# Second feed-forward of a fused graph network: 64-column scan matrices, pooling sums inside the value products, slice transposes in two banks

## The chip, the cores and the metric

The kernel runs on one core of a Trainium2 chip. The time is the device time of one execution in microseconds (us). Of the engines, TensorE (PE) makes matrix products and transposes, with weight loads (PEld) that overlap them; VectorE (DVE) and ScalarE (ACT) do elementwise work and read PE's results from eight PSUM banks; GpSimd (POOL) makes a few elementwise operations; SyncE (SP) issues transfers.

## The reference

Four layers, each a graph part and a feed-forward part, run over 32 graphs of 256 nodes with 128 features, all in fp32. The change lies in the feed-forward of the third layer (L2). For each graph, rows are softly assigned to 64 slices per head; the slices' means pass a two-way state-space scan (Hydra), and are spread back to the rows:

```python
sw = softmax((xm @ W_slice.T + b_slice) / temp)        # rows x 64 slices, 8 heads
snorm = sw.sum(2)
st = einsum('bhnc,bhng->bhgc', fx, sw) / (snorm + 1e-05)[..., None]
...                                                    # Hydra over the 64 slices of one graph:
h = h * dA_t[:, :, None, None] + dBx_t                 # forward, and on the flipped sequence
y = pad(y_fw[:, :-1], ((0, 0), (1, 0), (0, 0))) + pad(y_bw[:, 1:], ((0, 0), (0, 1), (0, 0)))
y = y + x_og * repeat(x_og @ fcD_w.T + Dp, P, axis=-1)
yg = y * silu(z)
yg = yg * rsqrt(mean(square(yg), -1, keepdims=True) + 1e-05) * norm_w
ot = yg @ out_w.T
out = einsum('bhgc,bhng->bhnc', ot, sw) @ out_w.T + out_b
```

No scan couples two graphs.

## The kernel before

`phase_ffn2` handles 512 rows, two graphs, in a turn; 16 turns (`every_turn`: the first two and the last two written out, the rest a loop of two). Every engine has a program of its own in written order, tied by semaphores; nothing is reordered. In a turn's program work of three turns is interleaved: the scan of turn t, the tail of turn t-1 (`tail_y`, `tail_o`, `tail_p`, `fin_piece`) and the softmax of turn t+1 (`to_features`, `lg_piece`, `soft_a`, `exp_piece`, `soft_b`).

The 128 partitions of a token tile are the 64 slices of graph a and the 64 of graph b. The scan is computed as a matrix: `dt_run` (dt times a mask, per direction) goes through a product with the masks (D, L2377, banks 6 and 7), exponentials (L2214) and a product with `factor` into `decay`, a 128x128 matrix per head of which only the two blocks of a row's own graph are not zero. `decay` times the tokens `xtok` gives y (L2387, bank 5).

Order on PE in a turn: `pool_h` (L2289), which waits for the previous turn's `yg`; `tail_y`; `pool_sums` for graph 0 (product with ones L2294 for the sums, value products L2296); `to_features`; `pool_sums` for graph 1; `tail_o` (L2263); `lg_piece` 0 (L2240); then z (L2332), which waits for `stT`; `lg_piece` 1; x (L2338); the rest of the projection; `lg_piece` 2, `tail_p`, `lg_piece` 3; `fin_piece` (L2282) and `swT_piece` (transposes of the slice weights, L2249, all through bank 0, evacuated by ACT L2145) in turns; the transposes of `xT` (L2363); G (L2368) and fcd (L2370); D; `swT_piece` 2, `fin_piece` 3; y; `swT_piece` 3.

Order on DVE: `pooled` for each graph (L2000, L2002, L2006); `soft_a` 0 (L1985), `soft_b` 0, `soft_a` 1, `sz`, `soft_b` 1; the convolution taps (L2020, L2026); the softplus of dt; `xT`, `Bt`, `Cpad`; `soft_a` 3; `dt_run` backward (L2086; ACT makes the forward one, L2203); `dt_both`, `gm`, `g8`, `g_both`, `factor` (L2098); `soft_b` 2; `decay` (L2104); the residual of turn t-1; the sum with `term` (L2110); `yg` (L2111); `soft_b` 3; `yn`.

Of the kernel before, what the change touches and what calls it, by code (L numbers as in the profile page):

```python
# [26 lines left out]
P = 128  # L27
# [1823 lines left out]
def phase_ffn2(nc, c):  # L1851
# [13 lines left out]
    LG = (B[3], B[2])  # L1865

# [8 lines left out]
    with ExitStack() as ctx:  # L1875
# [3 lines left out]
        def sem(n):  # L1879
# [9 lines left out]
        logit_w, value_w = sb("logit_w", [P, IN2]), sb("value_w", [P, IN2])  # L1889
        sn = sb("sn", [P, 2, KC, SL])  # L1890
# [9 lines left out]
        gm, g_both = sb("gm", [P, 2, P]), sb("g_both", [P, P])  # L1900
        xtok = sb("xtok", [P, IN2])

        dt_run = [sb(f"dt_run{i}", [P, HEADS2, P]) for i in range(2)]
        dt_both, factor = sb("dt_both", [P, HEADS2, P]), sb("factor", [P, HEADS2, P])
        decay = [c.spare["ffn2"][:, q * 4 * P:(q + 1) * 4 * P].rearrange("p (h t) -> p h t", h=4) for q in range(2)]
# [18 lines left out]
        with nc.Block() as block:  # L1924
            @block.gpsimd
            def _(g):
                def turn(t, par, first, last):
# [4 lines left out]
                    g.wait_ge(norm_ps, t * 2 + 1)  # L1932
# [10 lines left out]
            def _(v):  # L1943
# [30 lines left out]
                v.scalar_tensor_tensor(value_w[:], w["b_fx"], last_row, B[4][:], ALU.mult, ALU.add).then_inc(fused, 1)  # L1974
# [59 lines left out]
                def turn(t, par, first, last):  # L2034
# [3 lines left out]
                    pooled(t, 0)  # L2038
                    pooled(t, 1)
# [58 lines left out]
                    v.tensor_tensor(factor[:], dt_both[:], g_both[:, None, :].broadcast_to([P, HEADS2, P]), ALU.mult).then_inc(factor_ready, 1)  # L2098
# [26 lines left out]
            def _(a):  # L2125
# [43 lines left out]
                def turn(t, par, first, last):  # L2169
# [56 lines left out]
            def _(pe):  # L2226
# [84 lines left out]
                def turn(t, par, first, last):  # L2311
# [22 lines left out]
                    if more:  # L2334
                        lg_piece(t + 1, 1)
# [1130 lines left out]
```

## Time and profile before

| | us |
|---|---|
| runs | 3245.23, 3245.34, 3250.94; median 3245.34 |
| span of the profiled execution | 3243.7 |
| PE busy in the span | 2606.3 |
| DVE busy | 2274.7 |
| ACT busy | 1783.4 |
| a steady turn of this stage (14 of 16 are alike but for the clock) | 41.3 |

The profile's times count from the first instruction. The profiled execution is one by itself, whose only time is its span, 1.6 us under the runs' median. PE's busy time is modelled at a product's end, so a group's length holds the last product's tail. In a turn the distance between the same instruction of two turns is the cost of a turn; what the distance consists of has to be read from the waits between engines.

### The profile page before, as it was taken

What the parts mean: (1) busy time and instruction counts of PE and PEld (TensorE: products, weight loads), DVE (VectorE), ACT (ScalarE), POOL (GpSimd) and SP (SyncE); (2) the same over time, 40 slices, a digit from 0 to 9 for tenths busy, and PEclk for the clock granted to TensorE, in tenths of its full rate; (3) what the DMA queues carried; (4) which work ended last, traced back from release to release, by engine and by line L of the source; (5) the groups of instructions that cost most, each with busy time, mean ns of one, the idle gap of its engine ahead of it and who ended that gap; (6) DMA issues with size and microseconds to landing.
All of it is one profiled execution on the core that took longest, in us unless ns stands there. A gap on an engine that the chain in (4) does not pass through costs nothing. (4 is left out here: it accounts for less than half of the span.)

```text
span 3243.7 us, 68706 instructions
## 1 busy us (share of the span) xinstructions
PE 2606.3 (80%) x19386; PEld 2087.8 (64%) x19386; DVE 2274.7 (70%) x6679; ACT 1783.4 (55%) x5130; POOL 867.6 (27%) x863
## 2 busy tenths in 40 slices
PE   5899996992776941789999999699996888759992
PEld 4577776992675941656776777566664555549992
DVE  6777774666685656667777777499997688835555
ACT  2344434663674532755565555377774777726664
POOL 0233334663343432300000000000001155534442
PEclk9899997996887975989999999799998999969996
DMA  5111112334321213200000000000001000012225
GB/s 200 46 59 59 59 34 76 84 84 127 125 77 48 66 59 118 82 1 1 0 0 0 0 0 1 22 21 21 24 19 67 5 28 28 29 42 65 63 62 175
DMA packets 142548, 168.55 MB, mean 52 GB/s; under 512 B 19920, under 2 KB 118224, under 8 KB 141776
## 3 DMA queue, kind: packets, MB, share of 16 engines
q1 hardware_dynamic: 116688, 118.67, 12.1%
q0 software_dynamic: 21504, 44.74, 4.0%
q10 hardware_dynamic: 4224, 3.59, 0.4%
q8 instruction: 58, 0.95, 0.1%
q14 instruction: 74, 0.61, 0.1%
HBM read 115.87 MB, written 51.05 MB: 51 GB/s over the span
## 5 line engine op out<-in xcount | busy, mean ns | idle before, releaser
L1198 POOL DMA_INDIRECT y_rows<-ffn_e_rows_out,ffn_e_scatter_at x352 | 339.7, 965 | 385.7 <-DVE ffn_e_rows_out L1226 218.4
L1340 PE MATMUL bank<-ffn_e_xT,ffn_e_mine 128*128 128x128 f32 x3360 | 439.6, 278 | 2.2 <-ACT ffn_e_xT L1272 1.4
L1340 PEld LDWEIGHTS bank<-ffn_e_xT,ffn_e_mine 128*128 128x128 f32 x3360 | 410.4, 195 | 3.4 <-ACT ffn_e_xT L1272 2.2
L722 POOL DMA_INDIRECT sorted_rows<-ffn_rows,ffn_slot x320 | 315.5, 986 | 278.8 <-issue 266.4
L1274 ACT ACTIVATE ffn_e_mine<-constants 128x512 f32 (+1 forms) x352 | 250.2, 712 | 114.6 <-issue 65.3
L1246 DVE TENSOR_TENSOR ffn_e_hid<-ffn_e_act,bank 128x256 f32<-128x256 f32 (+1 forms) x280 | 136.1, 486 | 225.0 <-ACT ffn_e_act L1300 199.8
L1350 PE MATMUL bank<-ffn_e_mine,ffn_e_hid 128*128 128x128 f32 x1968 | 278.0, 276 | 2.6 <-DVE ffn_e_hid L1250 2.4
L2566 ACT ACTIVATE gnn_prob<-bank,gnn_low 128x256 f32<-128x256 f32 x512 | 203.5, 501 | 107.1 <-DVE gnn_low L2480 107.1
L1350 PEld LDWEIGHTS bank<-ffn_e_mine,ffn_e_hid 128*128 128x128 f32 x1968 | 247.5, 192 | 5.3 <-DVE ffn_e_hid L1250 4.8
L1300 ACT ACTIVATE ffn_e_act<-bank 128x256 f32<-128x256 f32 (+1 forms) x280 | 120.9, 432 | 106.0 <-PE bank L1340 104.9
L2480 DVE TENSOR_REDUCE gnn_low<-bank 128x2 f32<-128x512 f32 x256 | 159.0, 684 | 24.1 <-PE bank L2665 21.3
L2491 DVE SCALAR_TENSOR_TENSOR gnn_probT<-gnn_adj,bank 128x512 f32<-128x512 f32 x256 | 163.7, 681 | 7.2 <-PE bank L2677 3.7
L2140 ACT ACTIVATE bank<-bank,f_low 128x64 f32<-128x64 f32 x512 | 148.3, 296 | 36.8 <-DVE f_low L1985 36.8
L932 POOL TENSOR_TENSOR ffn_r_rstd<-ffn_r_var,minus_half 128x4 f32<-128x4 f32 x48 | 49.9, 1039 | 411.6 <-DVE ffn_r_var L820 348.8
L1234 DVE TENSOR_SCALAR ffn_e_mine<-constants 128x256 f32 (+2 forms) x352 | 126.6, 363 | 44.5 <-PE bank L1350 30.3
L2677 PE MATMUL bank<-ident,gnn_prob 128*128 128x128 f32 x1024 | 141.7, 278 | 4.1 <-DVE gnn_probT L2491 3.8
L2677 PEld LDWEIGHTS bank<-ident,gnn_prob 128*128 128x128 f32 x1024 | 111.8, 141 | 39.4 <-ACT gnn_prob L2566 25.2
L1937 POOL TENSOR_TENSOR f_term<-f_xtok,f_g 128x512 f32<-128x512 f32 x16 | 16.7, 1042 | 438.3 <-DVE f_g L2093 438.3
L1448 ACT ACTIVATE ffn_c_y<-ffn_c_y,ffn_gate 128x128 f32<-128x128 f32 x192 | 61.0, 389 | 129.5 <-DMA ffn_c_y<-y_rows 129.4
L2464 POOL TENSOR_TENSOR X<-X,constants 128x512 f32 (+1 forms) x16 | 17.4, 1089 | 356.7 <-ACT gnn_h L2585 356.7
L3002 ACT ACTIVATE att_prob<-bank,att_low 128x128 f32<-128x128 f32 (+1 forms) x256 | 105.6, 432 | 11.5 <-DVE att_low L2882 11.5
L2140 ACT ACTIVATION_READ_ACCUMULATOR bank<-bank,f_low 128x1 f32 x512 | 111.1, 217 | 0.2
(505 smaller groups left out, 6583.6 us busy)
## 6 DMA issues: line engine op xcount, KB each, us to landing
g_adj<-in_adjT SPq DMA_DIRECT2D x48, 512.0 KB, 4.0
ffn_e_rows_in<-sorted_rows SPq DMA_DIRECT2D x346, 66.0 KB
ffn_c_y<-y_rows SPq DMA_DIRECT2D x80, 256.0 KB, 3.2
g_adj_rows<-in_adj SPq DMA_DIRECT2D x16, 512.0 KB, 4.3
gnn_adj<-in_adjT SPq DMA_DIRECT2D x16, 512.0 KB, 4.0
constants<-in_ffn SPq DMA_DIRECT2D x1, 6281.0 KB, 22.2
y_rows<-ffn_e_rows_out,ffn_e_scatter_at POOLq DMA_INDIRECT x352, 2.2
constants<-in_ffn SPq DMA_DIRECT2D x1, 5204.0 KB, 15.4
```

Of the source, the lines that this page charges most:

```text
L722: eng.indirect_dma_start(c.sorted_rows, bass.IndirectOffsetOnAxis(r.slot[par][:, k, j:j + 1], 0), r.rows[par][:, j, :], None).then_inc(r.d ...
L1198: g.indirect_dma_start(c.y_rows, bass.IndirectOffsetOnAxis(scatter_at[par][:, k:k + 1], 0), rows_out[par][:, k, :], None).then_inc(scatter ...
L1234: v.tensor_scalar(mine3[place][:].rearrange("p (e c d) -> p e c d", e=1, c=NCH), w3[:, ds(e, 1), :, :], 1.0, None, ALU.mult).then_inc(seco ...
L1246: v.tensor_tensor(hid[k][:], act[k % 2][:], up, ALU.mult).then_inc(hid_ready, 1)
L1274: a.activation(mine1[place][:, None, :], w1[:, ds(e, 1), :], ACT.Copy).then_inc(first_copied, 1)
L1340: ins = pe.matmul(chunk(part, ch), chunk(weights[:, i * HALF:(i + 1) * HALF], ch), x, start=True, stop=True)
L1350: ins = pe.matmul(B[6 + par][:, k * D:(k + 1) * D], chunk(hid[k][:], ch), chunk(mine3[k][:], ch), start=(ch == 0), stop=(ch == NCH - 1))
L2140: ins = a.activation(lg, lg, ACT.Exp, bias=low[k % 2][:, hd:hd + 1], scale=-1.0, accum_out=sm[k % 2][:, hd:hd + 1])
L2480: v.tensor_reduce(low[q % 2][:, j, :], S[j].rearrange("p (q k) -> p q k", q=2), AX.X, ALU.min).then_inc(low_ready, 1)
L2491: v.scalar_tensor_tensor(probT[q % 2][:, j, :, :], adj[par][:, 2 * g:2 * g + 2, :], 1e-6, T_BANK[j % 2].rearrange("p (k q) -> p k q", k=2) ...
L2566: ins = a.activation(prob[q % 2][:, j, qt, :], S[j][:, qt * NODES:qt * NODES + NODES], ACT.Exp, bias=low[q % 2][:, j, qt:qt + 1], scale=-1.0)
L2677: ins = pe.transpose(T_BANK[j % 2][:, col:col + P], prob[q % 2][:, j, qt, kt * P:kt * P + P], c.ident[:])
```

## The change

The scan's matrices keep 64 columns, a row's own graph, in place of 128: `own_masks` is the sum of the masks' two halves, `dt_run` of both directions is made in one DVE operation (ACT's copies go), D is two products into bank 6 alone, the exponentials and `decay` cover 512 columns in all. G is four products of 64x64, now behind fcd, and y sixteen products of 64x64, eight heads for one graph and then eight for the other, with two slice transposes ahead of each eight.

The product with ones goes. `value_w` gets two forms: half of its 128 columns hold a head's value weights, the other half ones, so that one group of value products (`pool_values`) gives values and sums at once, for both graphs. `pooled` runs once a turn, over 512 columns. `lg_piece` 1 moves ahead of z. The slice transposes alternate between banks 0 and 7, and POOL's add of `out_b` waits for the value products.

```diff
@@ -1863,6 +1863,7 @@
...
+    SWT = (B[0], B[7])
...
@@ -1897,27 +1898,26 @@
...
+        own_masks, gm, g_both = sb("own_masks", [P, 2, SL]), sb("gm", [P, 2, SL]), sb("g_both", [P, SL])
-        dt_run = [sb(f"dt_run{i}", [P, HEADS2, P]) for i in range(2)]
-        dt_both, factor = sb("dt_both", [P, HEADS2, P]), sb("factor", [P, HEADS2, P])
-        decay = [c.spare["ffn2"][:, q * 4 * P:(q + 1) * 4 * P].rearrange("p (h t) -> p h t", h=4) for q in range(2)]
+        dt_run = sb("dt_run", [P, 2, HEADS2, SL])
+        dt_both, factor, decay = (sb(n, [P, HEADS2, SL]) for n in ("dt_both", "factor", "decay"))
...
@@ -1929,7 +1929,7 @@
...
-        g.wait_ge(norm_ps, t * 2 + 1)
+        g.wait_ge(st_ps, now)
...
@@ -1971,7 +1971,12 @@
...
-    v.scalar_tensor_tensor(value_w[:], w["b_fx"], last_row, B[4][:], ALU.mult, ALU.add).then_inc(fused, 1)
+    for a in range(2):
+        mine, bias = (ap.rearrange("p (k a s) -> p k a s", k=KC, a=2)[:, :, a, :] for ap in (B[4][:], w["b_fx"]))
+        v.tensor_copy(value_w[:, a, :, (1 - a) * SL:(2 - a) * SL], ones[:, None, 0:SL].broadcast_to([P, KC, SL]))
+        ins = v.scalar_tensor_tensor(value_w[:, a, :, a * SL:(a + 1) * SL], bias, last_row, mine, ALU.mult, ALU.add)
+    ins.then_inc(fused, 1)
+    v.tensor_tensor(own_masks[:], masks[:, :, 0:SL], masks[:, :, SL:], ALU.add)
...
@@ -1990,21 +1995,16 @@
...
-    def pooled(t, g):
-
-        n = (t * 2 + g) * 2
-        v.wait_ge(norm_ps, t * 2 + g + 1)
-        num, den = (B[4 + 2 * g + i][:].rearrange("p (k a s) -> p k a s", k=KC, a=2) for i in range(2))
-        for a in range(2):
-            rows_ = slice(a * HD2, (a + 1) * HD2)
-            ins = v.tensor_scalar(sn[rows_, g], den[rows_, :, a, :], 1e-5, None, ALU.add)
-        then(v, ins, stn, n + 1)
-        then(v, v.reciprocal(sn[:, g], sn[:, g]), stn, n + 2)
-        v.wait_ge(st_ps, t * 2 + g + 1)
-        for a in range(2):
-            rows_ = slice(a * HD2, (a + 1) * HD2)
-            ins = v.tensor_tensor(stT[rows_, :, g, :], num[rows_, :, a, :], sn[rows_, g], ALU.mult)
-        ins.then_inc(stT_ready, 1)
+    def pooled(t):
+
+        v.wait_ge(st_ps, t + 1)
+        low_half, high_half = slice(0, SL), slice(SL, P)
+        v.tensor_scalar(sn[low_half], B[5][high_half, :], 1e-5, None, ALU.add)
+        then(v, v.tensor_scalar(sn[high_half], B[7][low_half, :], 1e-5, None, ALU.add), stn, 2 * t + 1)
+        then(v, v.reciprocal(sn[:], sn[:]), stn, 2 * t + 2)
+        tokens = stT[:].rearrange("p k g s -> p (k g s)")
+        v.tensor_tensor(tokens[low_half], B[5][low_half, :], sn[low_half], ALU.mult)
+        v.tensor_tensor(tokens[high_half], B[7][high_half, :], sn[high_half], ALU.mult).then_inc(stT_ready, 1)
...
@@ -2083,26 +2082,23 @@
...
-        v.tensor_tensor(dt_run[1][:], per_head(dt[:, HEADS2:2 * HEADS2], P),
-                        masks[:, 1, None, :].broadcast_to([P, HEADS2, P]), ALU.mult).then_inc(dt_back_ready, 1)
-        v.wait_ge(dt_fwd_ready, t + 1)
-        v.wait_ge(dt_back_ready, t + 1)
-        v.tensor_tensor(dt_both[:], dt_run[0][:], dt_run[1][:], ALU.add).then_inc(dt_both_ready, 1)
+        v.tensor_tensor(dt_run[:], dt[:].rearrange("p (d h) -> p d h", d=2)[:, :, :, None].broadcast_to([P, 2, HEADS2, SL]),
+                        own_masks[:, :, None, :].broadcast_to([P, 2, HEADS2, SL]), ALU.mult).then_inc(dt_run_ready, 1)
+        v.wait_ge(dt_run_ready, t + 1)
+        v.tensor_tensor(dt_both[:], dt_run[:, 0], dt_run[:, 1], ALU.add).then_inc(dt_both_ready, 1)
...
-        v.tensor_tensor(gm[:], B[4][:, 0:2 * P].rearrange("p (a n) -> p a n", a=2), masks, ALU.mult).then_inc(gm_ready, 1)
+        v.tensor_tensor(gm[:], B[4][:, 0:2 * SL].rearrange("p (a n) -> p a n", a=2), own_masks[:], ALU.mult).then_inc(gm_ready, 1)
...
-        v.tensor_tensor(factor[:], dt_both[:], g_both[:, None, :].broadcast_to([P, HEADS2, P]), ALU.mult).then_inc(factor_ready, 1)
+        v.tensor_tensor(factor[:], dt_both[:], g_both[:, None, :].broadcast_to([P, HEADS2, SL]), ALU.mult).then_inc(factor_ready, 1)
...
-        for half in range(2):
-            v.wait_ge(D_exp, t * 2 + half + 1)
-            v.tensor_tensor(decay[half], B[6 + half][:].rearrange("p (a n) -> p a n", a=4),
-                            factor[:, half * 4:half * 4 + 4, :], ALU.mult).then_inc(decay_ready, 1)
+        v.wait_ge(D_exp, t + 1)
+        v.tensor_tensor(decay[:], heads(B[6][:]), factor[:], ALU.mult).then_inc(decay_ready, 1)
...
@@ -2198,21 +2194,16 @@
...
-        a.wait_ge(dt_ready, t + 1)
-        for hd in range(HEADS2):
-            ins = a.activation(dt_run[0][:, hd, :], masks[:, 0, :], ACT.Copy, scale=dt[:, hd:hd + 1])
-        ins.then_inc(dt_fwd_ready, 1)
...
-        for half in range(2):
-            a.wait_ge(D_ps, t * 2 + half + 1)
-            for k in range(4):
-                one = B[6 + half][:, k * P:(k + 1) * P]
-                ins = a.activation(one, one, ACT.Exp, scale=neg_a[:, half * 4 + k:half * 4 + k + 1])
-            ins.then_inc(D_exp, 1)
+        a.wait_ge(D_ps, t + 1)
+        for hd in range(HEADS2):
+            one = B[6][:, hd * SL:(hd + 1) * SL]
+            ins = a.activation(one, one, ACT.Exp, scale=neg_a[:, hd:hd + 1])
+        ins.then_inc(D_exp, 1)
...
@@ -2239,15 +2230,21 @@
...
+    def swT_part(par, k, chunks):
+
+        for j in chunks:
+            ins = pe.transpose(SWT[k % 2][:, j * P:(j + 1) * P], sw[par][:, k, j * P:(j + 1) * P], c.ident[:])
+        return ins
+
...
-        wait_past(pe, swT_ready, t * TT + k)
-        for j in range(KC):
-            ins = pe.transpose(B[0][:, j * P:(j + 1) * P], sw[par][:, k, j * P:(j + 1) * P], c.ident[:])
-        ins.then_inc(swT_ps, 1)
+        if k == 1:
+            pe.wait_ge(stT_ready, t + 1)
+        wait_past(pe, swT_ready, t * TT + k - 1)
+        swT_part(par, k, range(KC)).then_inc(swT_ps, 1)
...
@@ -2289,12 +2286,14 @@
...
-    def pool_sums(t, g):
-        pe.wait_ge(ph_ready, t * 2 + g + 1)
-        mm(B[5 + 2 * g][:], ones[:], pooled_h[:, g, :], start=True, stop=True).then_inc(norm_ps, 1)
-        for j in range(KC):
-            ins = mm(B[4 + 2 * g][:, j * P:(j + 1) * P], value_w[:, j * P:(j + 1) * P], pooled_h[:, g, j * P:(j + 1) * P],
-                     start=True, stop=True)
+    def pool_values(t):
+
+        pe.wait_ge(ph_ready, t * 2 + 2)
+        wait_past(pe, swT_ready, t * TT)
+        for a in range(2):
+            for j in range(KC):
+                cols = slice((2 * j + a) * SL, (2 * j + a + 1) * SL)
+                ins = mm(B[5 + 2 * a][:, j * P:(j + 1) * P], value_w[:, a, j, :], pooled_h[:, :, cols], start=True, stop=True)
...
@@ -2316,23 +2315,21 @@
...
-        pool_sums(t, 0)
...
-        pool_sums(t, 1)
+        pool_values(t)
...
-        pe.wait_ge(stT_ready, t * 2 + 2)
+            lg_piece(t + 1, 1)
+        pe.wait_ge(stT_ready, t + 1)
...
-        if more:
-            lg_piece(t + 1, 1)
...
@@ -2364,30 +2361,35 @@
...
+        for k in range(KC):
+            mm(B[4][:, 2 * P:2 * P + HEADS2], xT[:, k, :], fcd[:, k, :], start=(k == 0), stop=(k == KC - 1))
...
-            ins = mm(B[4][:, d * P:(d + 1) * P], Bt[:], Cpad[:, 2 * d:2 * d + P], start=True, stop=True)
-        for k in range(KC):
-            ins = mm(B[4][:, 2 * P:2 * P + HEADS2], xT[:, k, :], fcd[:, k, :], start=(k == 0), stop=(k == KC - 1))
+            for g in range(2):
+                ins = mm(B[4][g * SL:(g + 1) * SL, d * SL:(d + 1) * SL], Bt[:, g * SL:(g + 1) * SL],
+                         Cpad[:, 2 * d + g * SL:2 * d + (g + 1) * SL], start=True, stop=True)
...
-        pe.wait_ge(dt_fwd_ready, t + 1)
-        pe.wait_ge(dt_back_ready, t + 1)
-        for half in range(2):
-            for d in range(2):
-                ins = mm(B[6 + half][:], masks[:, 1 - d, :], dt_run[d][:, half * 4:half * 4 + 4, :].rearrange("p a n -> p (a n)"),
-                         start=(d == 0), stop=(d == 1))
-            ins.then_inc(D_ps, 1)
+        pe.wait_ge(dt_run_ready, t + 1)
+        for d in range(2):
+            ins = mm(B[6][:], masks[:, 1 - d, :], dt_run[:, d].rearrange("p h n -> p (h n)"), start=(d == 0), stop=(d == 1))
+        ins.then_inc(D_ps, 1)
...
-        for hd in range(HEADS2):
-            if hd % 4 == 0:
-                pe.wait_ge(decay_ready, t * 2 + hd // 4 + 1)
-            ins = mm(B[5][:, hd * HD2:(hd + 1) * HD2], decay[hd // 4][:, hd % 4, :], xtok[:, hd * HD2:(hd + 1) * HD2],
-                     start=True, stop=True)
-        ins.then_inc(y_ps, 1)
-        swT_piece(t, par, 3)
+        pe.wait_ge(decay_ready, t + 1)
+
+        def product_y(g):
+            rows_ = slice(g * SL, (g + 1) * SL)
+            for hd in range(HEADS2):
+                cols = slice(hd * HD2, (hd + 1) * HD2)
+                ins = mm(B[5][rows_, cols], decay[rows_, hd, :], xtok[rows_, cols], start=True, stop=True)
+            return ins
+        wait_past(pe, swT_ready, t * TT + 2)
+        swT_part(par, 3, (0, 1))
+        product_y(0)
+        swT_part(par, 3, (2, 3)).then_inc(swT_ps, 1)
+        product_y(1).then_inc(y_ps, 1)
...
```

What stands on PE around the pooling, in a written-out turn: before,

```order
L2256 MATMUL bank<-ident,f_yn 128x128 x4
L2294 MATMUL bank<-f_pooled_h,f_ones 128x512
L2296 MATMUL bank<-f_pooled_h,f_value_w 128x128 x4
L2233 MATMUL bank<-ident,f_h 128x128 x4
L2294 MATMUL bank<-f_pooled_h,f_ones 128x512
L2296 MATMUL bank<-f_pooled_h,f_value_w 128x128 x4
L2263 MATMUL bank<-f_ygT,constants 128x128 x16
L2240 MATMUL bank<-f_logit_w,f_hT 128x512
L2332 MATMUL bank<-constants,f_stT 128x512 x4
L2240 MATMUL bank<-f_logit_w,f_hT 128x512
```

and now (`f_yn` feeds tail_y, `f_h` to_features, `f_stT` the projection z):

```order
L2253 MATMUL bank<-ident,f_yn 128x128 x4
L2224 MATMUL bank<-ident,f_h 128x128 x4
L2296 MATMUL bank<-f_pooled_h,f_value_w 128x128 x8
L2260 MATMUL bank<-f_ygT,constants 128x128 x16
L2231 MATMUL bank<-f_logit_w,f_hT 128x512 x2
L2331 MATMUL bank<-constants,f_stT 128x512 x4
```

The two products with ones are gone, the value products stand in one group behind to_features, and both first products of the softmax stand ahead of z.

PE at the end of a turn, from G on: before,

```order
L2368 MATMUL bank<-f_Cpad,f_Bt 128x128 x2
L2370 MATMUL bank<-constants,f_xT 128x8 x4
L2377 MATMUL bank<-f_dt_run,constants 128x512 x4
L2249 MATMUL bank<-ident,f_sw 128x128 x4
L2282 MATMUL bank<-constants,f_swT 128x128 x4
L2387 MATMUL bank<-f_xtok,constants 128x64 x8
L2249 MATMUL bank<-ident,f_sw 128x128 x4
```

and now:

```order
L2365 MATMUL bank<-constants,f_xT 128x8 x4
L2368 MATMUL bank<-f_Cpad,f_Bt 64x64 x4
L2374 MATMUL bank<-f_dt_run,constants 128x512 x2
L2236 MATMUL bank<-ident,f_sw 128x128 x4
L2279 MATMUL bank<-constants,f_swT 128x128 x4
L2236 MATMUL bank<-ident,f_sw 128x128 x2
L2386 MATMUL bank<-f_xtok,f_decay 64x64 x8
L2236 MATMUL bank<-ident,f_sw 128x128 x2
L2386 MATMUL bank<-f_xtok,f_decay 64x64 x8
```

D halves, y doubles in number, and the last slice transposes moved from behind y to two places inside it.

## Rows read from the trace of the kernel before

**Rows 1.** Windows by turn: length; busy PE, weight loads, DVE, ACT, POOL; clock; DMA.
```profile
1597.95:1639.25 41.30, 38.75 (x237) 29.15 (x237) 32.51 (x78) 24.74 (x103) 2.87 (x3) 1.00 0.00 0
...
1721.90:1765.00 43.10, 40.60 (x237) 29.91 (x238) 32.46 (x78) 24.59 (x103) 2.87 (x3) 0.96 0.00 0
```

**Rows 2.** Timeline, PE, first half: start, length (us), line, operands, passes [idle <- releaser].
```profile
1597.92 3.67 PE L2289 MATMUL bank<-f_sw,f_h 128*128 128x512 f32 x8 [1.20 <-issue]
...
1601.87 1.02 PE L2294 MATMUL bank<-f_pooled_h,f_ones 128*128 128x512 f32 x2
...
1605.81 3.74 PE L2263 MATMUL bank<-f_ygT,constants 128*128 128x128 f32 x32
1609.38 1.02 PE L2240 MATMUL bank<-f_logit_w,f_hT 128*128 128x512 f32 x2
1610.24 3.60 PE L2332 MATMUL bank<-constants,f_stT 128*128 128x512 f32 x8
...
1614.53 3.73 PE L2338 MATMUL bank<-f_stT,constants 128*128 128x128 f32 x32
```

**Rows 3.** Timeline, DVE, first half of the same turn.
```profile
1602.93 0.86 DVE L2000 TENSOR_SCALAR f_sn<-bank 64x256 f32<-64x256 f32 x2 [2.28 <-PE bank L2294]
1603.82 1.75 DVE L2002 RECIPROCAL f_sn<-f_sn 128x256 f32<-128x256 f32 x1
...
1610.44 0.69 DVE L1985 TENSOR_REDUCE f_low<-bank 128x8 f32<-128x512 f32 x1 [0.41 <-PE bank L2240]
...
1618.93 0.86 DVE L2020 TENSOR_SCALAR f_xc<-f_xpad,constants 128x128 f32<-128x128 f32 x3
```

**Rows 4.** Timeline, PE, second half of the same turn.
```profile
1626.96 0.66 PE L2249 MATMUL bank<-ident,f_sw 128*128 128x128 f32 x4 [1.18 <-ACT f_swT L2145]
...
1628.34 0.60 PE L2363 MATMUL bank<-ident,f_xT 128*128 128x128 f32 x4
1628.87 0.71 PE L2368 MATMUL bank<-f_Cpad,f_Bt 64*128 64x128 f32 x4
...
1630.43 3.68 PE L2377 MATMUL bank<-f_dt_run,constants 128*128 128x512 f32 x8
...
1635.55 1.97 PE L2387 MATMUL bank<-f_xtok,constants 128*128 128x64 f32 x16
...
1639.21 3.69 PE L2289 MATMUL bank<-f_sw,f_h 128*128 128x512 f32 x8 [1.26 <-DVE f_yg L2111]
```

**Rows 5.** Timeline, DVE, second half of the same turn.
```profile
1628.73 1.23 DVE L2086 TENSOR_TENSOR f_dt_run<-f_dt,constants 128x1024 f32<-128x1024 f32 x1
...
1631.98 1.98 DVE L2098 TENSOR_TENSOR f_factor<-f_dt_both,f_g_both 128x1024 f32<-128x1024 f32 x1
...
1637.55 0.70 DVE L2110 TENSOR_TENSOR bank<-bank,f_term 128x512 f32<-128x512 f32 x1
1638.29 0.69 DVE L2111 SCALAR_TENSOR_TENSOR f_yg<-bank,f_sz 128x512 f32<-128x512 f32 x1
```

**Rows 6.** Timeline, ACT, second half of the same turn.
```profile
1630.35 0.27 ACT L2140 ACTIVATE bank<-bank,f_low 128x64 f32<-128x64 f32 x1
1630.55 0.20 ACT L2140 ACTIVATION_READ_ACCUMULATOR bank<-bank,f_low 128x1 f32 x1
```

**Rows 7.** Groups by line and shape: count; busy us, mean ns; idle before, releasers.
```profile
L2387 PEld LDWEIGHTS bank<-f_xtok,constants 128*128 128x128 f32 x256 | 29.9, 191 | 4.6 <-issue 3.8 <-DVE constants L2104 0.8
...
L2689 PEld LDWEIGHTS bank<-gnn_probT,gnn_v 128*32 128x32 f32 x1024 | 26.8, 109 | 39.0 <-issue 21.1 <-DVE gnn_probT L2491 5.2
...
L2065 DVE RECIPROCAL f_r<-f_e 128x16 f32<-128x16 f32 x16 | 4.0, 253 | 0.5
```

**Rows 8.** Timeline, PE, a later stage that uses 32-column tiles.
```profile
2301.45 1.07 PE L2689 MATMUL bank<-gnn_probT,gnn_v 128*32 128x256 f32 x16
```

**Rows 9.** Windows: before a fall of the clock; the same place undisturbed.
```profile
1718.50:1721.90 3.40, 2.15 (x20) 1.91 (x19) 3.18 (x10) 0.32 (x1) 0.00 (x0) 1.00 0.00 0
...
1635.44:1639.21 3.77, 2.41 (x20) 2.21 (x21) 3.55 (x10) 0.53 (x2) 0.00 (x0) 1.00 0.00 0
```

More of the change, by code:

```diff
@@ L1888, in phase_ffn2 @@
         ones, differ, neg_a = sb("ones", [P, P]), sb("differ", [P, P]), sb("neg_a", [P, 2 * HEADS2])
-        logit_w, value_w = sb("logit_w", [P, IN2]), sb("value_w", [P, IN2])
-        sn = sb("sn", [P, 2, KC, SL])
+        logit_w, value_w = sb("logit_w", [P, IN2]), sb("value_w", [P, 2, KC, P])
+        sn = sb("sn", [P, IN2])
         stT = sb("stT", [P, KC, 2, SL])
@@ L1899, in phase_ffn2 @@
             "dtr", "u", "m", "e", "e2", "r", "s", "s2", "poly", "dt"))
-        gm, g_both = sb("gm", [P, 2, P]), sb("g_both", [P, P])
+        own_masks, gm, g_both = sb("own_masks", [P, 2, SL]), sb("gm", [P, 2, SL]), sb("g_both", [P, SL])
         xtok = sb("xtok", [P, IN2])
-        dt_run = [sb(f"dt_run{i}", [P, HEADS2, P]) for i in range(2)]
-        dt_both, factor = sb("dt_both", [P, HEADS2, P]), sb("factor", [P, HEADS2, P])
-        decay = [c.spare["ffn2"][:, q * 4 * P:(q + 1) * 4 * P].rearrange("p (h t) -> p h t", h=4) for q in range(2)]
+        dt_run = sb("dt_run", [P, 2, HEADS2, SL])
+        dt_both, factor, decay = (sb(n, [P, HEADS2, SL]) for n in ("dt_both", "factor", "decay"))
         g8, term, yg, yn = sb("g8", [P, HEADS2]), sb("term", [P, IN2]), sb("yg", [P, IN2]), sb("yn", [P, IN2])
@@ L1911, in phase_ffn2 @@
         (setup, filled, differ_ready, wx_ready, fused_ps, fused, a_exp, h_ready, hT_ps, hT_ready, ph_ps, ph_ready, lg_ps,
-         weights, lg_ready, lg_exp, sw_ready, norm_ps, st_ps, stn, stT_ready, z_ps, tz_ready, sz_ready, x_ps, xpad_ready, bcd_ps, bcd_ready, conv,
+         weights, lg_ready, lg_exp, sw_ready, st_ps, stn, stT_ready, z_ps, tz_ready, sz_ready, x_ps, xpad_ready, bcd_ps, bcd_ready, conv,
          xc_ready, bc_ready, tx_ready, tbc_ready, xT_ready, bct_ready, sp, spm_ready, spe_ready, dt_ready, G_ps,
-         gm_ready, g_both_ready, xt_ps, xtok_ready, g8_ready, term_ready, dt_fwd_ready, dt_back_ready, dt_both_ready, factor_ready, D_ps, D_exp,
+         gm_ready, g_both_ready, xt_ps, xtok_ready, g8_ready, term_ready, dt_run_ready, dt_both_ready, factor_ready, D_ps, D_exp,
          decay_ready, y_ps, y_sum, yg_ready, ms_ready, ve_ready, rstd_ready, yn_ready, yT_ps, ygT_ready, ot_ps,
@@ L1917, in phase_ffn2 @@
              "setup filled differ_ready wx_ready fused_ps fused a_exp h_ready hT_ps hT_ready ph_ps ph_ready lg_ps "
-             "weights lg_ready lg_exp sw_ready norm_ps st_ps stn stT_ready z_ps tz_ready sz_ready x_ps xpad_ready bcd_ps bcd_ready conv "
+             "weights lg_ready lg_exp sw_ready st_ps stn stT_ready z_ps tz_ready sz_ready x_ps xpad_ready bcd_ps bcd_ready conv "
              "xc_ready bc_ready tx_ready tbc_ready xT_ready bct_ready sp spm_ready spe_ready dt_ready G_ps "
-             "gm_ready g_both_ready xt_ps xtok_ready g8_ready term_ready dt_fwd_ready dt_back_ready dt_both_ready factor_ready D_ps D_exp "
+             "gm_ready g_both_ready xt_ps xtok_ready g8_ready term_ready dt_run_ready dt_both_ready factor_ready D_ps D_exp "
              "decay_ready y_ps y_sum yg_ready ms_ready ve_ready rstd_ready yn_ready yT_ps ygT_ready ot_ps "
@@ L2037, in turn @@
                         all_but_last(1, h[1]).then_inc(h_ready, 1)
-                    pooled(t, 0)
-                    pooled(t, 1)
+                    pooled(t)
                     if more:
@@ L2144, in swT_piece @@
                     a.wait_ge(swT_ps, t * TT + k + 1)
-                    a.activation(swT[:, k], B[0][:].rearrange("p (j n) -> p j n", j=KC), ACT.Copy).then_inc(swT_ready, 1)
+                    a.activation(swT[:, k], SWT[k % 2][:].rearrange("p (j n) -> p j n", j=KC), ACT.Copy).then_inc(swT_ready, 1)
                 evac_hT(0)
```

## The prediction

> **What bounds the kernel now.** I read the windows by turn first. The change touches only the second feed-forward stage, which runs 16 turns of 512 rows; a steady turn takes 41.30 us with TensorE (PE) busy for 38.75 of them [rows 1], which looks like a TensorE bound. The timelines of one turn say otherwise. In the first half PE runs without a break [rows 2], but the Vector engine (DVE) starts the next turn's softmax search (L1985) only 0.41 us after its pooling arithmetic ends [rows 3], so two chains arrive there almost together. From L1985 to the first convolution tap (L2020) there are 8.49 us of DVE and Scalar-engine (ACT) alternation, and from there to dt_run (L2086) another 9.80 us of DVE [rows 3, 5]. In the second half the path is dt_run on DVE and ACT, the D product (L2377), the exponentials (L2214), decay, the y product (L2387), then the sum with term (L2110) and yg (L2111), for which the next turn's first product waits 1.26 us [rows 4, 5]. So PE is nearly full but sets the end only in parts. What the stage takes is counted between two starts of L2289: 15 such distances and a last turn.
>
> An fp32 product shows as two passes, a transpose as one. 32 passes of 128 columns take 3.57 us, 0.112 each [rows 2]; a 512-column pass takes about 0.43 (L2240's two end 1.02 after the first began) [rows 2].
>
> **Pooling.** The two products with ones go, four passes of 0.43 us, 1.7 us of PE. The value products stay at 16 passes of 0.112, now in one group. From a turn's first pass to the end of tail_y there are 1601.87-1597.92 = 3.95 us [rows 2]; then 4 transposes 0.44, the 16 passes 1.79, 0.16 for the last one's tail and 0.04 to DVE: DVE begins its pooling 6.38 us into the turn, where before it began at 5.01 with the first graph [rows 2, 3]. DVE then does everything in one go: two adds and two multiplies of 512 columns and one reciprocal of 512. A 512-column operation takes 0.69 (L1985) to 0.70 (L2110) [rows 3, 5]; reading other partitions than it writes is new, and the upper bound is that of two 256-column ones, 0.86 [rows 3]. The reciprocal took 0.253 us for 16 columns and 1.75 for 256 [rows 3, 7], 6.24 ns a column, so 3.35 for 512 (upper bound twice 1.75 = 3.50; below, the 256-column price per column less a tenth, 3.15). Sum 4 x 0.70 + 3.35 + 0.10 of gaps = 6.25; it ends 12.63 into the turn. Before, L1985 began at 12.52 [rows 2, 3]. So pooling is **+0.1 us a turn** (bounds -0.2 to +0.9), and the 1.7 us of PE are not gained: the z product (L2332) needs the same result, and PE, through with tail_o and two lg products by 11.5, waits there some 1.3 us. The L1985-to-L2020 chain hides nothing, it just starts 0.1 later; x, which ended 8.0 us after z began before [rows 2] and now loses the lg product between them, still lands before it ends.
>
> **Slice transposes in two banks.** The 1.18 us wait for ACT's evacuation in front of the second L2249 goes [rows 4]. What is next on PE is the transpose of xT (L2363), and xT comes from the unbroken DVE chain that ends in dt_run; PE now arrives about 1.2 us earlier and waits for that. Worth 0.
>
> **Scan, first part.** ACT's eight dt_run copies go; DVE makes both directions in one operation, 1024 elements as before, 1.23 us [rows 5]. G's four small products (8 passes) replace 4 passes and come behind fcd; both lie beside dt_run, so 0. D halves to two products, 4 passes: 3 x 0.43 + 0.59 = 1.88 us instead of two such groups. The eight exponentials have 64 columns: two commands of that shape follow each other in 0.20 us [rows 6], so 8 x 0.20 + 0.10 = 1.70. ACT's softmax exponentials in front of them end before D does. Decay is one operation of 512, 0.69. dt_both, gm, g_both and factor halve on DVE. Factor took 1.98 where dt_run, of the same size, took 1.23 [rows 5]; while GpSimd makes term it may cost 0.7 to 1.4, and DVE still reaches decay about when the exponentials end (cover 0.1 us; gone, it costs up to 0.5).
>
> **Scan, y.** Eight products become sixteen on half the rows and half the columns: 32 passes, all of one half in the same corner of the array, with two transposes in front of each half. The old 16 passes of 64 columns took 1.97, no less per pass than those of 128 columns (0.112) [rows 2, 4], so the weight load sets the price. A load of 128 columns takes 191 ns, of 32 columns 109 [rows 7]: 0.85 ns a column, so 64 columns load 55 ns faster and a pass costs 0.112-0.055 = 0.057. The lower bound continues to 32 columns, 0.030; the upper is no gain, 0.112. I take 0.057, because load time fell with columns in the one other shape that shows it. A change of array shape: four transposes begin at 1628.34, the next pass would come at 1628.78 and the 64-row one comes at 1628.87 [rows 4], 0.09, and I take 0.12 because the first load is not hidden either. y block: 4 x 0.11 + 32 x 0.057 + 3 x 0.12 + 0.16 = 2.78 us (bounds 1.9 to 4.6). The slice transposes in it lay behind y before, beside DVE's work; now half of them stand in front of y's end.
>
> Sum from the start of dt_run to the start of the sum with term, hand-over from DVE to PE taken as 0.15 (between 0.04, PE to DVE at L1985, and 0.23, yg to L2289 [rows 2 to 5]): 1.23 + 0.15 + 1.88 + 0.04 + 1.70 + 0.04 + 0.69 + 0.15 + 2.78 + 0.04 = 8.70. Before: 1637.55-1628.73 = 8.82 [rows 5]. **-0.1 us a turn.** Residual and statistics on DVE (1.7 us) fit beside the block. The path is even: 15 x (0.1-0.1) = 0. Setup has four operations for value_w in place of one and a mask sum: +1 us, once.
>
> **The clock.** Most turns run at granted 1.00 (2.4 GHz). One turn shows 0.96 and takes 43.10, 1.8 us more [rows 1]; two more like it lie in the stage. There the clock fell to 1.2 GHz right behind a stretch of 3.40 us in which PE was busy 2.15; in an undisturbed turn the same place, from the end of the last fin product to the next L2289, is 3.77 us with 2.41 busy [rows 9]. After the change: counted from dt_run's start, D's passes end at 3.1, swT and fin at 4.4; PE waits for decay until 5.9 (1.4 idle), runs the block until 8.5, and waits for yg until 8.7 + 1.66 = 10.4 (1.9 idle). That is 6.0 us with some 2.6 busy, a longer and emptier place than the one that now ends in a fall in 3 turns. I take a fall in 10 of the 15: 7 more x 1.8 = **+12.6 us** (ends: no more, 0; each turn, +22).
>
> The Trainium skill ("TensorE: Matmul & The Clock Gate", HAM oscillation) has the clock fall back to half behind idle gaps between bursts of matmuls, and means longer gaps than any in this stage. By that rule no turn would fall, before or after, and the sum would lack the 12.6 us: 3246, the time of the first rival below. The trace differs: the clock fell where no gap was longer than about 1.3 us.
>
> **Total.** The runs' median is 3245.34 us; the profiled execution has a span of 3243.7 us, 1.6 less, and I put the sum on the median: 3245.3 + 0 + 1 + 12.6 = **3259 us**.
>
> **Rivals.**
> - *Even path, clock as now.* The freed PE time is only waited out at xT, z and decay, and the emptier place brings no more falls: 3245.3 + 1 = 3246. For it: idle of 1.2 us twice a turn mostly does no harm today. Against: the 6.0 us above. 0.22.
> - *Faster: small passes cheaper.* At 0.030 a pass the y block loses 0.9 us a turn, 13 us, with some more falls (+5): 3238; without them 3233. It decides below about 0.045 a pass. For it: passes that lie in four different parts of the array come at 1.07 us for 16 passes of 256 columns [rows 8]. Against: here neighbours lie in the same corner and full transposes stand between the corners. 0.18. The Trainium skill (same page, Part 3, packing small matmuls) lets products in different row and column groups run concurrently; by it the two halves of y would overlap and give this same saving if the transposes were not between them.
> - *Slower: small passes at full price.* At 0.112 the block is 4.5 us, 1.75 more a turn, 26 us; with the clock between today's and my count: 3272 to 3285. For it: 64 columns cost what 128 do in [rows 4], and every split product has a first load of its own. It decides above 0.07. 0.18.
> - *The forecast*, 0.42.
>
> **How the numbers follow.** What a measurement of this kernel can tell from no change is about 0.2%, 6.5 us. Slower: forecast and full price, 0.42 + 0.18, less 0.02 of the forecast for few falls, 0.58; within: the even path and that remainder, 0.24; faster: 0.18. The range leaves out a tenth on either side: from the cheap passes with falls, a little below 3238, to the full price with falls, a little above 3285: 3236 to 3288.
>
> **What would show it.** Right: z waits for stT about 1.3 us, xT's transposes wait for DVE, PE idles before decay and yg, turns of 41.3 us among turns of 43 and more, PEclk of the stage below 1.00 in most of them. Right for y: 32 passes some 0.06 apart, and L2110's successor about 8.7 us behind dt_run. Wrong: a reciprocal far from 3.35, exponentials not 0.20 apart, passes at 0.03 or 0.11, or a clock that holds at 1.00 through the emptier turns.

## The result, and the profile after

The changed kernel takes 3275.8 us (median of 4 runs) where the kernel before takes 3245.8: ratio 1.0097, 95% interval 1.0080 to 1.0115, **30 us slower**. The forecast was 3259 us, 13.6 slower; the time lies inside the stated range, but the loss is 16 us larger than forecast.

The windows by turn of the changed kernel (columns as in [rows 1]) show three turns with falls of the granted clock (from 2.4 to 1.2 GHz for a few us: at both places told below, at pool_h alone, at D alone) and the only one of the 15 without:

```profile
1565.82:1609.84 44.02, 39.36 (x248) 29.17 (x249) 29.78 (x71) 21.54 (x95) 2.86 (x3) 0.92 0.00 0
1609.84:1652.88 43.04, 37.65 (x248) 28.25 (x249) 29.87 (x73) 21.82 (x95) 2.86 (x3) 0.96 0.00 0
1652.88:1695.23 42.35, 37.66 (x248) 28.54 (x249) 29.79 (x71) 21.55 (x95) 2.87 (x3) 0.96 0.00 0
1953.13:1994.31 41.18, 35.95 (x248) 27.69 (x249) 29.76 (x72) 21.68 (x95) 2.87 (x3) 1.00 0.00 0
```

At clock 1.00 a turn is 41.18 us, no longer than before (41.30), with PE busy 2.8 us less. The other turns behind the first are 42.35 to 44.5 us long. The PE timeline of the turn at 1.00, its second half, against [rows 4]:

```profile
1982.78 0.66 PE L2360 MATMUL bank<-ident,f_xT 128*128 128x128 f32 x4 [0.83 <-DVE f_xT L2075]
1983.27 1.06 PE L2365 MATMUL bank<-constants,f_xT 128*128 128x8 f32 x8
1984.26 0.45 PE L2368 MATMUL bank<-f_Cpad,f_Bt 64*64 64x64 f32 x8
1985.22 1.95 PE L2374 MATMUL bank<-f_dt_run,constants 128*128 128x512 f32 x4 [0.51 <-DVE f_dt_run L2085]
1987.01 0.60 PE L2236 MATMUL bank<-ident,f_sw 128*128 128x128 f32 x4
1987.45 1.06 PE L2279 MATMUL bank<-constants,f_swT 128*128 128x128 f32 x8
1989.83 0.41 PE L2236 MATMUL bank<-ident,f_sw 128*128 128x128 f32 x2 [1.32 <-issue]
1990.17 1.14 PE L2386 MATMUL bank<-f_xtok,f_decay 64*64 64x64 f32 x16
1991.24 0.44 PE L2236 MATMUL bank<-ident,f_sw 128*128 128x128 f32 x2
1991.61 1.14 PE L2386 MATMUL bank<-f_xtok,f_decay 64*64 64x64 f32 x16
1994.31 3.67 PE L2286 MATMUL bank<-f_sw,f_h 128*128 128x512 f32 x8 [1.56 <-issue]
```

The path is as worked out: y block 1989.83 to 1992.75, and waits ahead of xT, D, decay and the next pool_h. In a turn with falls the same two groups, D and pool_h, are longer: D by 1.1 us, pool_h by 1.7 (PE timeline). The windows over the low stretches show 0.50, that is 1.2 GHz:

```profile
1685.01 3.08 PE L2374 MATMUL bank<-f_dt_run,constants 128*128 128x512 f32 x4 [0.51 <-DVE f_dt_run L2085]
...
1695.23 5.37 PE L2286 MATMUL bank<-f_sw,f_h 128*128 128x512 f32 x8 [1.56 <-issue]
```
```profile
1685.70:1689.11 3.41, 3.41 (x9) 1.79 (x9) 2.66 (x6) 1.51 (x9) 1.04 (x1) 0.50 0.00 0
1695.92:1699.33 3.41, 3.41 (x5) 1.35 (x5) 1.93 (x7) 1.05 (x2) 0.55 (x1) 0.50 0.00 0
```

Where the 27.7 us between the two spans lie, by the starts of pool_h: ahead of the stage -0.8; first turn +5.0; the next 14 turns 582.81 to 601.43, +18.6; the last turn and all behind it +4.9. Of the 15 pool_h behind the first one, 9 are long in this way (3 before), and of the 15 D, 9 (before none). In the last turn a third place joins them: z, behind a wait of 2.72 us, takes 5.29 us where a z at full clock takes 3.70 (PE timeline). The first turn follows it (windows, before and after):

```profile
2051.11 5.29 PE L2331 MATMUL bank<-constants,f_stT 128*128 128x512 f32 x8 [2.72 <-DVE f_stT L2007]
```
```profile
1381.23:1431.07 49.84, 37.47 (x153) 23.22 (x152) 32.08 (x74) 24.34 (x120) 2.31 (x2) 0.83 0.00 1
```
```profile
1380.43:1435.28 54.85, 37.84 (x166) 24.13 (x164) 29.39 (x68) 21.42 (x112) 2.31 (x2) 0.75 0.00 1
```

### The profile page after: what moved, and what is told of

The parts are those of the page before. It is cut to its first block and busy times, and to the rows that moved or that the text cites. A ratio compares the mean times of both kernels' runs of the same rounds, so it can differ in the third digit from the quotient of the medians.

```text
span 3271.4 us, 68778 instructions
## 1 busy us (share of the span) xinstructions
PE 2597.2 (79%) x19578; PEld 2082.1 (64%) x19578; DVE 2231.6 (68%) x6587; ACT 1737.0 (53%) x5002; POOL 868.2 (27%) x863
```

## The experiments

**Theory A**: the path is even, and the time is lost at the lower granted clock, which comes because PE has too little to do in parts of a turn. **Rival B**: the chain of a turn itself became longer. The first run decides: it gives PE dummy products and changes nothing else.

*Dummies in the changed kernel.*

```diff
+def filler(bank, n):
+    mm(bank[:, 0:n], c.ident[:], in_w[:, 0, 0:n], start=True, stop=True)
...
+filler(B[4], 384)
 pe.wait_ge(stT_ready, t + 1)
...
+pe.wait_ge(xpad_ready, t + 1)
+filler(B[5], 256)
 pe.wait_ge(xT_ready, t + 1)
...
+filler(B[6], 128)
 pe.wait_ge(dt_run_ready, t + 1)
...
+filler(B[5], 512)
 pe.wait_ge(decay_ready, t + 1)
...
 product_y(1).then_inc(y_ps, 1)
+pe.wait_ge(swT_ready, t * TT + 3)
+filler(B[0], 512)
+filler(B[0], 256)
```

> The changed kernel with dummy products on TensorE (the identity times a block of in_w; nobody reads what they write) in five places of a turn where it waits: ahead of z (384 columns), ahead of the xT transposes (256), ahead of D (128), ahead of the decay wait (512) and behind the y products (768). No product of the kernel is left out and no engine but TensorE gets work. Theory A (the granted clock): the changed path is as long as the one before, 41.35 against 41.28 us in a turn, and what was lost is the time at the lower granted clock, which fell in nearly every turn because TensorE has too little to do between its waits. Then the falls of the steady stage (19) go to 3 or fewer, the turns come at 41.2 to 41.6 us, and the time is 3243 to 3252 us. Theory B (a longer chain: the turns are longer because work on the path itself grew, and the fall of the clock is only seen beside it): the time stays at 3270 to 3285 us, the turns at 42.5 us or more. Between these: the dummies stand in the way of the products behind them by 0.1 to 0.2 us in a turn each, then 3255 to 3262 us at a full clock.

3246.4 us, ratio to before 0.9995 (0.9986 to 1.0004). The whole loss is gone. In the trace no pool_h behind the first is long any more, and two D are. A turn, by windows:

```profile
1764.84:1806.09 41.25, 39.85 (x261) 29.46 (x261) 29.87 (x73) 21.82 (x95) 2.86 (x3) 1.00 0.00 0
```

PE has more to do, and the turns are 1 to 3 us shorter; that leaves B no room. Theory A holds.

*Dummies in the kernel before.*

```diff
+pe.wait_ge(xpad_ready, t + 1)
+filler(B[5], 512)
 swT_piece(t, par, 1)
...
 swT_piece(t, par, 3)
+filler(B[7], 512)
```

> The kernel before with two dummy products of 512 columns in a turn (results nobody reads): one on TensorE ahead of the second slice transpose, behind the convolution's pads, and one behind the last slice transpose. Theory A (the granted clock costs time in the kernel before too): its three falls in the steady stage, 1.7 to 1.95 us each, go, and the time is 3239 to 3242 us. Theory B (the falls are hidden, or dummies cost as much as they give): 3245 to 3249 us.

3236.3 us, 0.9961 (0.9947 to 0.9975), below the range of theory A: no fall is left from the second turn to the last but one, and turns are 41.1 to 41.3 us (window of one). The kernel before paid for its clock too: 10.7 us in the medians of the runs taken together (3246.95 to 3236.3), 4.2 in the profiled spans, of which that of the dummies is its slowest run's.

```profile
1844.49:1885.77 41.28, 40.47 (x240) 29.64 (x241) 32.46 (x79) 24.69 (x103) 2.86 (x3) 1.00 0.00 0
```

*Which part brings the falls.* Parts of the change's diff, put into the kernel before: the pooling alone; the scan and the two banks without it; the 64-column scan alone, with `SWT = (B[0], B[0])` and the waits for that one bank.

> The kernel before with the pooling part of the change alone: the sums of the softmax come out of the value products (an interleaved weight with blocks of ones), one reciprocal of 512 columns, one wait ahead of z; scan and slice transposes as before. Theory A1 (the clock falls come mostly from the pooling stage, where TensorE loses two products of sums and waits 1 us more ahead of z): the path grows by 0.2 us in a turn (3 us in all), the setup by 1 to 4 us, and falls at the following pool_h in half the turns or more cost 10 to 15 us: 3258 to 3268 us. Theory A2 (the falls come from the scan, whose passes were halved): the clock falls as rarely as before, 3 times or so: 3248 to 3253 us. Theory B (the pooling's chain is itself what is longer, by over 1 us a turn): 3260 us or more with the clock at its full level.

> The kernel before with the other two parts of the change: scan matrices of 64 columns and slice transposes in two banks; the pooling as before. Theory A2 (the falls come from the scan, where TensorE has half the passes left): the path is 0.1 to 0.2 us a turn shorter, the clock falls in 8 turns of 15 or more at 1.1 to 1.9 us each: 3256 to 3268 us. Theory A1 (the falls come from the pooling stage): three falls or so as before, 3240 to 3246 us. Theory B (a longer chain in the scan): 3255 us or more with the clock at its full level.

> The kernel before with the scan matrices of 64 columns alone: pooling as before, and the slice transposes in one bank with their waits as before (the last slice's transposes stand between the halves of y, as in the change). The scan with two banks took 3289 us. Theory S (halving the scan's passes is what lowers the clock): 3278 to 3292 us, with a fall in every turn. Theory T (the slice transposes, which no longer wait and so leave the idle time in one piece ahead of xT, are what lowers it): 3244 to 3252 us.

| kernel | us | ratio to before (95%) |
|---|---|---|
| pooling alone | 3244.8 | 0.9994 (0.9983 to 1.0005) |
| scan alone | 3266.1 | 1.0062 (1.0046 to 1.0078) |
| scan and banks | 3289.3 | 1.0125 (1.0110 to 1.0141) |
| all three (the change) | 3275.8 | 1.0097 (1.0080 to 1.0115) |

The pooling costs nothing by itself: two long pool_h and, in the last turn, one long D, as rarely as A2 has it, and a time 3 us below A2's range, since its turns are 0.1 us shorter (41.15) where I had given it 0.1 to 0.2 more. The scan brings falls, and the two banks add to them, some 22 us (each kernel against the runs of the kernel before taken with it), though what they do is take a wait away. For scan and banks that is 21 us more than A2's range has, and the scan alone lies between S and T, so neither the scan's passes nor the bank is the whole of it. Scan alone has 9 long pool_h and no long D; with the second bank all 15 pool_h are long, and 3 D. The parts don't add up: the pooling on top of scan and banks takes 12 us off, and why was not tested. With scan and banks, from the fifth turn on, nearly all of pool_h runs at 1.2 GHz, and the turns are 44.3 to 44.5 us, one like the other (PE timeline, window of that turn):

```profile
1785.80 6.72 PE L2288 MATMUL bank<-f_sw,f_h 128*128 128x512 f32 x8 [1.56 <-issue]
```
```profile
1785.80:1830.25 44.45, 40.37 (x253) 29.57 (x253) 30.83 (x78) 22.03 (x95) 2.86 (x3) 0.92 0.00 0
```

*Which idle place decides.* Of the five dummies above, those of the scan alone (xT, `dt_run`, decay), and the two behind y alone.

> The changed kernel with the dummy products of the scan alone (256 columns ahead of the xT transposes, 128 ahead of D, 512 ahead of the decay wait; nobody reads them); nothing ahead of z and nothing behind the y products. Theory A3 (each fall has its own place: idle time in the scan lowers the clock at D, the idle 1.7 us before yg lowers it at the next pool_h): the falls at D go and those at pool_h stay, some 8 to 10 of 1.7 us: 3258 to 3266 us. Theory A4 (it is the scan's idle time that brings both, since its work stands just ahead of the wait for yg too): 3246 to 3252 us, with 4 falls or fewer in the 15 turns.

> The changed kernel with the dummy products behind the y products alone (512 and 256 columns, in the wait for yg). Theory A3 (each fall has its own place): the falls at pool_h go and those at D stay, 8 to 10 of 1.1 us: 3254 to 3262 us. Theory A4 (the scan's idle time brings both): little is gained, 3266 to 3276 us. A third outcome, 3246 to 3250 us, would say that the wait for yg alone decides and that the falls at D are an echo of it.

The scan's three: 3280.5 us, 1.0109 (1.0092 to 1.0125), no gain, against A3 and A4 alike; the clock is still low at D in 11 turns of 15, with a dummy right in front of it, and at pool_h in 14. Those behind y: 3253.0 us, 1.0029 (1.0018 to 1.0039); no pool_h is long any more, and of the 9 long D two are left. So it is nearly the third outcome, 3 us above it. PE timelines, first of the scan's dummies, then of those behind y:

```profile
1819.82 0.49 PE L2300 MATMUL bank<-constants,ident 128*128 128x128 f32 x2
1820.31 3.47 PE L2380 MATMUL bank<-f_dt_run,constants 128*128 128x512 f32 x4
...
1831.04 5.30 PE L2286 MATMUL bank<-f_sw,f_h 128*128 128x512 f32 x8 [1.70 <-DVE f_yg L2107]
```
```profile
1760.52 1.95 PE L2377 MATMUL bank<-f_dt_run,constants 128*128 128x512 f32 x4 [0.51 <-DVE f_dt_run L2085]
...
1767.98 1.56 PE L2300 MATMUL bank<-constants,ident 128*128 128x512 f32 x4
1769.61 3.67 PE L2286 MATMUL bank<-f_sw,f_h 128*128 128x512 f32 x8
```

*The same dummies behind y with scan and banks, and work of the kernel's own in that place.* The diff is that of the second kernel, which moves transposes; the third adds one dummy at its end.

```diff
-swT_piece(t, par, 2)
 fin_piece(t - 1, 3)
+wait_past(pe, swT_ready, t * TT + 1)
+swT_part(par, 2, (0, 1))
...
-wait_past(pe, swT_ready, t * TT + 2)
-swT_part(par, 3, (0, 1))
+swT_part(par, 2, (2,))
 product_y(0)
-swT_part(par, 3, (2, 3)).then_inc(swT_ps, 1)
+swT_part(par, 2, (3,)).then_inc(swT_ps, 1)
 product_y(1).then_inc(y_ps, 1)
+swT_piece(t, par, 3)
```

> The scan and the two banks without the pooling (3289 us) with dummy products of 512 and 256 columns behind the y products, in the wait for yg. Theory E: the 18 falls of the steady stage go and the turns come from 44.4 to 41.1 to 41.4 us: 3240 to 3250 us. Rival (in this kernel the turns are longer by work on the path): 3275 us or more.

> The changed kernel without any dummy: the transposes of the third slice (two, one, one) take the places of the last slice's around the halves of y, and the last slice's four stand behind y, in the wait for yg, as in the kernel before. Theory E (what TensorE has to do between the decay wait and the next pool_h decides on the clock, as the run with dummies there alone suggests): 0.5 us of work of the kernel's own comes into that wait and the falls become rare: 3244 to 3256 us. Rival (only more work than the kernel has to place there helps, or the work taken from ahead of the decay wait is missed as much): 3265 to 3285 us. The path itself gets 0.2 us a turn shorter either way, 3 us in all.

> The same with one dummy product of 512 columns (nobody reads it) behind the four transposes, in the wait for yg. Theory E: falls nearly gone, turns of 40.9 to 41.1 us as in the run with five dummies and two transposes moved: 3235 to 3242 us. Rival (dummies in the scan are needed too): 3255 us or more.

Theory E was too simple. Scan and banks with dummies: 3262.3 us (3248.8 to 3266.2), 27 us better, but not at 3250, so between E and its rival; the other two land in the ranges of their rivals. The moved transposes: 3269.0 us (3264.4 to 3275.4), 1.0070; with one dummy, 3262.7 us, the runs spread from 3249.1 to 3266.8. What was moved were transposes, one pass each, where the dummies are products; whether the two weigh alike for the clock was not tested. The trace with the moved transposes shows how such a spread can come about (windows of two turns): it has five turns of 43.9 to 45.4 us in a row, with low clock in each, and right behind them six of 41.0 to 41.2 with none.

```profile
1656.61:1700.84 44.23, 39.47 (x249) 29.09 (x249) 29.80 (x71) 21.62 (x95) 2.86 (x3) 0.92 0.00 0
1954.62:1995.65 41.03, 36.11 (x249) 27.77 (x249) 29.77 (x72) 21.76 (x95) 2.86 (x3) 1.00 0.00 0
```

*Two candidates for a better kernel.* First all five dummies (now 256 columns ahead of decay and 512 and 128 behind y; the other three as before) with two transposes taken out of the y block; then the pooling with the two dummies that the kernel before had.

```diff
+wait_past(pe, swT_ready, t * TT + 2)
+swT_part(par, 3, (0, 1))
 pe.wait_ge(xtok_ready, t + 1)
+filler(B[5], 256)
 pe.wait_ge(decay_ready, t + 1)
...
-wait_past(pe, swT_ready, t * TT + 2)
-swT_part(par, 3, (0, 1))
+swT_part(par, 3, (2,))
 product_y(0)
-swT_part(par, 3, (2, 3)).then_inc(swT_ps, 1)
+swT_part(par, 3, (3,)).then_inc(swT_ps, 1)
 product_y(1).then_inc(y_ps, 1)
+pe.wait_ge(swT_ready, t * TT + 3)
+filler(B[0], 512)
+filler(B[0], 128)
```

> The changed kernel with dummy products (nobody reads them) in all five places and the first two transposes of the last slice moved ahead of the decay wait, so that one transpose instead of two stands before each half of y. With dummies alone the change took 3246.4 us. If the two transposes were on the path, they take 0.2 us off each of 16 turns: 3242 to 3244 us, and with the falls that were left in that run (three, 1.5 us each) gone, 3239 to 3242 us. If the moved work leaves TensorE too idle near y, the clock falls again: 3255 us or more. If the chain does not run through y here: 3246 us.

> The kernel before with the pooling of the change and two dummy products of 512 columns, one ahead of the second slice's transposes and one behind the last slice's. With the dummies alone the kernel before took 3236.3 us, with the pooling alone 3244.8 us. If the pooling shortens the path by 0.1 us a turn, as its trace has it (41.0 and 41.3 us against 41.16 and 41.41), the two add up: 3233 to 3236 us. If the wait ahead of z that it brings costs the clock again: 3240 to 3246 us.

The first takes 3237.8 us, 0.9974 (0.9965 to 0.9984): faster than both kernels, at 40.9 to 41.0 us a turn, one at 41.3 (window of one turn). The two transposes were on the path (0.2 us a turn; the smaller dummies were not, for with the larger ones PE still waited 0.42 us for decay and up to 0.2 for yg). What the rest of the 8.6 us to the five dummies alone consists of was not taken apart; two D of that run are long, here none.

```profile
1807.11:1848.03 40.92, 39.25 (x261) 29.61 (x261) 29.78 (x71) 21.55 (x95) 2.87 (x3) 1.00 0.00 0
```

The second takes 3243.3 us, 0.9992 (0.9983 to 1.0001), a miss: its turns came at 41.0 to 41.3 as expected, but the last distance between two yg is 41.1 us instead of the 38.9 of the kernel before. There z starts 0.5 us later with the new pooling, and the clock is low in z (window in that turn). What else lies between it and the 3236 us of dummies alone wasn't found.

```profile
2022.20:2025.40 3.20, 3.20 (x5) 1.35 (x4) 0.00 (x0) 0.00 (x0) 0.00 (x0) 0.50 0.00 0
```

## Why the prediction was right and wrong

- *Pooling*: right. First pass to DVE's add 6.45 us (6.38 forecast), reciprocal 3.35 (3.35), the four others 0.68 to 0.69, soft_a 12.68 into the turn (12.63), z waits 1.00 for `stT` (1.3). DVE timeline, against [rows 3]:

```profile
1959.58 0.69 DVE L2002 TENSOR_SCALAR f_sn<-bank 64x512 f32<-64x512 f32 x1 [3.73 <-PE bank L2296]
1960.29 0.68 DVE L2003 TENSOR_SCALAR f_sn<-bank 64x512 f32<-64x512 f32 x1
1961.00 3.35 DVE L2004 RECIPROCAL f_sn<-f_sn 128x512 f32<-128x512 f32 x1
...
1965.81 0.69 DVE L1990 TENSOR_REDUCE f_low<-bank 128x8 f32<-128x512 f32 x1
```

- *Two banks*: path right, clock not thought of. The 1.18 us wait went and came back as 0.83 in front of xT, behind DVE. On the scan alone the second bank cost some 22 us, and not in the path, for scan and banks with dummies has turns of 41.3 to 41.4 us where no fall is: I had worked out that PE would wait ahead of xT instead, and put that at nothing.
- *Scan*: right. dt_run to the sum with term 8.94 us (8.70), D 1.95 (1.88), exponentials 1.72 (1.70), y block 2.92 (2.78). Sixteen 64x64 passes start within 0.92 us, 0.061 each (0.057), so both y rivals fall. DVE and ACT timelines, against [rows 5]:

```profile
1983.85 1.23 DVE L2085 TENSOR_TENSOR f_dt_run<-f_dt,f_own_masks 128x1024 f32<-128x1024 f32 x1
...
1992.79 0.70 DVE L2106 TENSOR_TENSOR bank<-bank,f_term 128x512 f32<-128x512 f32 x1 [1.43 <-PE bank L2386]
```
```profile
1987.21 1.72 ACT L2205 ACTIVATE bank<-bank,f_neg_a 128x64 f32<-128x64 f32 x8 [0.77 <-PE bank L2374]
```

The group of the weight loads answers to [rows 7]: 139 ns, where I took 191 less 55.

```profile
L2386 PEld LDWEIGHTS bank<-f_xtok,f_decay 64*64 64x64 f32 x506 | 33.1, 139 | 5.4 <-issue 5.4
```

- *Setup*: from the first product of the stage to its first pool_h 18.56 us, before 18.36: +0.2, where I took 1.
- *The clock*: **the step that failed is the size of this term**, "a fall in 10 of the 15: 7 more x 1.8", 12.6 us. It counts one place, pool_h behind the wait for yg, and for that place it came out right: 9 of the 15 fall, 6 more than before, at 1.7 each, about 10 us. What it puts at nothing is every other place. D falls in 9 of 15 turns at 1.1 us, another 10 us: the sum had no term for it. Which of PE's waits lowers the clock at D stays open, for dummies ahead of xT and of D did not keep it up (3280.5 us), and those behind y did (3253.0). The first turn loses 5.0 us, at clock 0.75 against 0.83, and the last one 4.9: 1.7 at pool_h, 1.6 at z, 1.1 at D, and 0.5 because z starts later there (its long pool_h and D are among the nines). By turns the sum is the same: in the 14 inner ones the low clock costs 601.4 - 14 x 41.18 = 25 us against 582.8 - 14 x 41.29 = 5 before. How much of the first turn's 5.0 is the clock stays open: with five dummies it is still 53.85 us.

The emptier place itself was sized well too: from the last fin product to the next pool_h 5.94 us with 2.92 busy (6.0 and 2.6 forecast; windows, against [rows 9]). That its count of 10 came so near 9 is in part luck, for it was a guess between none and all, and in other kernels of this case with the same scan the clock is low at pool_h in 15 turns or, for half the stage, in none:

```profile
1646.94:1652.88 5.94, 2.92 (x36) 2.42 (x37) 3.89 (x11) 1.15 (x5) 0.00 (x0) 1.00 0.00 0
```

The sentence that I had put against my own forecast, the Trainium skill's ("TensorE: Matmul & The Clock Gate", HAM oscillation), does not account for the steady turns: it has the clock fall behind idle gaps longer than any of theirs, where the longest wait on PE is 1.70 us, and the clock fell. My remark that it means longer gaps than any in the stage was wrong for the first and the last turn: PE waits up to 3.8 us there before, and up to 5.0 after, and the first turn has the lowest clock of all. Another section of that page (A second HAM failure mode: psum-queue depth-cycling) tells of a kernel whose many short idles between groups of products make the clock swing; the falls of the steady turns look more like that, though no run here shows that the cause is the same.

## What to carry to other kernels

Where an engine's granted clock falls in some turns already, work taken away beside the path may not be free: look at what the engine still does between its waits, in each place of a turn and in the first and last turn as well, before a freed microsecond is called a gain. Here the one place that was priced came out as forecast, and the places left at nothing cost as much again. When the low clock shows in the windows, a product whose result nobody reads, in the right wait, is the cheapest experiment, and here it turned 30 us of loss into none and took some 10 us off the kernel before. The right wait had to be found by runs: the same kind of dummies in the scan's waits gained nothing.

## What the runs showed of the hardware

- Falls come in series in some kernels: with scan and banks every turn behind the first is 44.3 to 44.65 us long, with the moved transposes six turns with low clock stand ahead of six without, at 41.0 to 41.2, in the same code. The runs of one kernel (moved transposes and a dummy) then spread over 18 us (3249 to 3267). That a turn lengthened by its falls brings the next ones on would fit, but the changed kernel has long D and long pool_h in turns about, and no run tests it. Why a dummy behind y also keeps the clock up at D, some 34 us later, wasn't shown either.
- A 64x64 fp32 pass takes 0.061 us where a 128x128 one takes 0.112; G's, which alternate between two parts of the array, started 8 within 0.23 us, 0.033 each, two by two 0.007 us apart.
- The second bank, whose one use is to take a wait of 1.18 us from PE, made the kernel with the scan alone some 22 us slower.
